# The corner block of a triangular inverse by two TensorE passes in two of the step bodies, and a rearranged first step

## The chip, the cores and the metric

The kernel runs on one core of a Trainium2 chip. The metric is the device time of one launch in microseconds, the median of several runs. All data are float32 unless a line says otherwise.

## The reference

One layer: a delta-rule attention over chunks, and behind it a mixture of experts with a shared part. What matters here is the first half, cut to the lines that the change touches:

```python
# q, k, v: silu of a causal convolution over 4 tokens of x @ W; beta = sigmoid(x @ Wb)
A = jnp.einsum('bhncd,bhnmd->bhncm', k_beta, k)
M = jnp.where(stril, A, 0.0) + jnp.eye(chunk)
u = solve_triangular(M, v_beta, lower=True)
w = solve_triangular(M, k_beta, lower=True)
def step(S, inp):
    u_i = u_i - w_i @ S
    o_i = q_i @ S + tril(q_i @ k_i.T) @ u_i
    S = S + k_i.T @ u_i
# B, T, D, H = 2, 1024, 512, 16; dk = 32
# then: norm of o by head, o @ Wo, residual; router, 32 experts with 4 of them per token, shared part, norms
```

The solves are with unit lower triangular matrices. The kernel takes chunks of 32 tokens, forms the inverse of each matrix once and multiplies by it.

## The kernel before

**Staging.** The tokens are taken in 8 steps of 128 tokens of both batches (256 columns). The program has a set-up part, body 0, bodies 1 to 8, a closing body 9, and then, behind a barrier of all engines, the expert part. Body s prepares step s on VectorE (DVE) and ScalarE (ACT): convolutions, silu, grams, and the inverses of its 128 x 4 triangular matrices. In the same body TensorE (PE) runs the core of step s-1: four sub-steps j = 0 to 3, each of a state matmul (L497), a solve (L512: inverse times residual), a state update (L520) and an output matmul (L526). Between these four, `fill` puts pieces of other work, written out by hand in `FILL` and `FILLS`: one letter is one piece, X turn of x, B betas, G one gram (L481), P half a projection (L468, step s+1), W output projection (L549, step s-2), O output squares (L539), R router, E and F first halves of the shared part, V and Y its second half, H turn of h. `FILL` has 16 slots; slot 4j+m stands behind operation m of sub-step j. Slot 13 is "PP", slot 14 is empty, slot 15 is "EEEEOEEEE". In bodies 1 and 7 the letters of steps that don't exist drop out: body 1 has no W, E, F, V, Y; body 7 has no X and P.

**The ring.** The pieces write to six PSUM banks in turn. `all_jobs` lists the jobs in TensorE's order, a job's bank is its number modulo 6, and `wait_free` waits until the job six before has been released.

**The inverse.** A matrix of 32 x 32 is held on each of the 128 partitions for each of the entries in `inv`. `masks` (L975) copies a gram from PSUM with the upper triangle kept, `problems` (L983) turns them, `row_weights` and `column_weights` scale, and `inverse_diagonal` (L1012) solves the two diagonal blocks of 16 x 16. The block below them, the corner, is minus the second inverse times the block times the first inverse: `turn_first` (L1021), `below_times_first` (L1032, products of 8 x 16 x 16 and 8 x 16 x 8) and `second_times` (L1038, the same sizes), each a product by `tensor_tensor` (L1028) and a sum by `tensor_reduce` (L1030) on VectorE. `inverse_by_token` (L1043) turns the result into `invT` and signals `inv_ready`, for which the solve of the next core waits at j = 0.

**The order at the end of a body** is fixed on VectorE: state j = 2, column weights, the copy of `turn_first`, moments of x, residual j = 3 (L1067), the two products of `below_times_first`, state j = 3 (L1071), turn of k, `output_sums` (L1077), the two products of `second_times`, `scale_output` (L1084), `inverse_by_token`; then residual j = 0 of the next body. On ScalarE: copies of projections and solves, the output's copy (L728) and square (L733), `output_norm` (L736).

**Body 0** has no core. TensorE projects step 0 (L633), waiting for `consts`, which GpSimd signals at the end of its constants; then betas, the four grams, the turn of x, and all twelve P. VectorE convolves k, takes moments, convolves q, multiplies k, turns it, scales x, multiplies q, convolves v, masks. ScalarE copies banks 0 to 3, then the sigmoid factor of k, bank 4, that of q, bank 5, moments, betas, that of v, x. At its end VectorE scales the output weights `wo` by `onw` (L1204).

Of the kernel before, what the change touches and what calls it, by code (L numbers as in the profile page):

```python
# [26 lines left out]
P = 128  # L27
# [33 lines left out]
PIECES = dict(X=1, H=1, O=1, G=4, P=12, W=8, E=8, F=8, V=4, Y=4)  # L61
BANKS = dict(X=2, H=2, O=2, G=4, P=6, W=2, E=2, F=2, V=1, Y=1)

FILL = ["BXRWW", "WWW", "WWW", "PP", "GPP", "GFF", "GFF", "GFF", "FFPP", "HPP", "PP", "VVVV", "YYYY", "PP", "", "EEEEOEEEE"]
FILLS = {0: ["BGGGGXPPPPPPPPPPPP"],
         STEPS: ["RWWW", "WWW", "WW", "F", "FF", "F", "F", "FF", "FH", "VV", "V", "VY", "YYY", "EE", "E", "EEOEEE"], STEPS + 1: ["RWWWWWWWWFFFFFFFFHVVVVrYYYYEEEEEEEE"]}


def step_of(body, section):

    if section in "XP":
        return body + 1
    if section in "BG":
        return body
    if section == "O":
        return body - 1
    if section in "WHEr":
        return body - 2
    return body - 3


def pieces_of(body):

    done = dict.fromkeys("BRrXHOGPWEFVY", 0)
# [29 lines left out]
class Ring:  # L114
# [17 lines left out]

    def full(self, *job):
# [6 lines left out]
def step_part(nc, ctx, dram, shared):  # L140
# [24 lines left out]
    upto = sb("upto", [P, CH])  # L165
    eps_l2 = sb("eps_l2", [P, 1])
# [25 lines left out]
    mid_cols = sig[:, 2, HB * HB:2 * HB * HB].rearrange("p (c j) -> p c j", c=HB)  # L192

# [66 lines left out]
    halo_done = sem("halo_done")  # L260
    kq_ready = sem("kq_ready")
# [34 lines left out]
    act_step = sem("act_step")  # L296

# [87 lines left out]
    def _(pool):  # L385
# [8 lines left out]
        g.memset(upto[:, :], 1.0)  # L394
        g.memset(pre[:, :, :, 0:HALO], 0.0)
# [37 lines left out]
    def _(pe):  # L433
# [39 lines left out]
        def gram(s, j):  # L473
# [9 lines left out]
            m.then_inc(ring.full("G", s, j), 1)  # L483

# [117 lines left out]
        def fill_for(body):  # L602
# [3 lines left out]
            def fill(at):  # L606
                for c, step, n in slots[at]:
# [10 lines left out]
                    elif c == "G":  # L618
                        gram(step, n)
                    elif c == "P":  # L620
# [23 lines left out]
    def _(act):  # L644
# [46 lines left out]
        def take_projection(s, n):  # L691
# [13 lines left out]
            release("P", s, n)  # L705
            if half == 1:
# [11 lines left out]
        def key_norms(s):  # L718
# [3 lines left out]
            sc_e.activation(knorm[:, :], knorm[:, :], ACT.Exp, scale=0.5).then_inc(knorm_ready, 1)  # L722

# [91 lines left out]
        for n in range(BANKS["P"]):  # L815
            take_projection(1, n)
        end_steps()

        def body(s):
# [10 lines left out]
            if new:  # L830
                silu_factor(s, 1)
                silu_factor(s, 0)
# [37 lines left out]
            if nxt:  # L870
                take_projection(s + 1, 5)
            take_output(core, 3)
# [79 lines left out]

# [912 lines left out]
```

## Time and profile before

| | |
|---|---|
| median of 3 runs | 963.0 us (961.36 to 964.35) |
| profiled execution | 962.78 us, its span 961.0 us |
| PE, weight loads, DVE, ACT, POOL busy | 822.5, 629.2, 661.5, 364.8, 116.7 us |
| mean granted clock of TensorE | 0.934 of full speed |
| body 0 | up to 86 us |
| body 1, first residual to first residual of body 2 | 85.96 to 155.75 us |
| body 7, in the same way | 536.62 to 611.84 us |
| expert part | from 703.4 us |

Times of rows are microseconds from the start of the span. Busy shares are of the whole span; what one stage waits for is read from the timelines. The time before an instruction in which its engine was idle stands in brackets at the end of its row, with what ended it; "issue" is idle time in which the engine waited for nothing that the profile shows.

### The profile page before, as it was taken

What the parts mean: (1) busy time and instruction counts of PE and PEld (TensorE: products, weight loads), DVE (VectorE), ACT (ScalarE), POOL (GpSimd) and SP (SyncE); (2) the same over time, 40 slices, a digit from 0 to 9 for tenths busy, and PEclk for the clock granted to TensorE, in tenths of its full rate; (3) what the DMA queues carried; (4) which work ended last, traced back from release to release, by engine and by line L of the source; (5) the groups of instructions that cost most, each with busy time, mean ns of one, the idle gap of its engine ahead of it and who ended that gap; (6) DMA issues with size and microseconds to landing.
All of it is one profiled execution on the core that took longest, in us unless ns stands there. A gap on an engine that the chain in (4) does not pass through costs nothing. (4 is left out here: it accounts for less than half of the span.)

```text
span 961.0 us, 30663 instructions
## 1 busy us (share of the span) xinstructions
PE 822.5 (86%) x13456; PEld 629.2 (65%) x13456; DVE 661.5 (69%) x1220; ACT 364.8 (38%) x683; POOL 116.7 (12%) x173
## 2 busy tenths in 40 slices
PE   6794779789999999999999787998779999999910
PEld 5683665676777777687687464666566887788800
DVE  2799699799789789879877988787691222222238
ACT  2605334435534644544554451332321222222215
POOL 2000000000000000000000000000002454544345
PEclk9895988999999999999999987998889999999965
DMA  8301004300101021020020020020176999999376
GB/s 307 72 23 47 3 3 168 108 3 25 62 18 39 3 69 27 24 70 23 4 69 24 3 70 23 2 89 2 48 286 220 362 362 346 344 360 358 96 266 278
DMA packets 49632, 113.09 MB, mean 118 GB/s; under 512 B 8688, under 2 KB 8816, under 8 KB 49504
## 3 DMA queue, kind: packets, MB, share of 16 engines
q1 hardware_dynamic: 44384, 100.70, 29.1%
q0 software_dynamic: 5120, 10.49, 4.8%
q8 instruction: 104, 1.70, 0.7%
q14 instruction: 24, 0.20, 0.1%
HBM read 84.34 MB, written 26.84 MB: 116 GB/s over the span
## 5 line engine op out<-in xcount | busy, mean ns | idle before, releaser
L468 PE MATMUL bank<-xnT,wring 128*128 128x256 f32 x768 | 183.6, 396 | 2.1 <-ACTq L681 1.3
L468 PEld LDWEIGHTS bank<-xnT,wring 128*128 128x128 f32 x768 | 149.3, 198 | 24.9 <-ACTq L681 1.5
L587 PE MATMUL bank<-late,ffn_w 128*128 128x256 f32 x480 | 117.3, 394 | 0.0
L1754 DVE TENSOR_TENSOR hid<-ps_g,sg 128x160 f32<-128x160 f32 x32 | 10.4, 324 | 148.5 <-ACT sg L1650 148.5
L942 DVE SCALAR_TENSOR_TENSOR cv<-pre,taps,cv 128x1024 f32<-128x1024 f32 x72 | 92.4, 1283 | 18.1 <-ACTq L707 14.4
L587 PEld LDWEIGHTS bank<-late,ffn_w 128*128 128x128 f32 x480 | 90.8, 195 | 15.2 <-issue 1.1
L1509 POOL MEMSET xgT<- 128x512 f32 x2 | 1.0, 532 | 686.9 <-POOLq L1834 686.9
L1609 PEld LDWEIGHTS ps_g<-xgT,wring 128*128 128x128 f32 x640 | 74.4, 192 | 10.9 <-issue 10.9
L1609 PE MATMUL ps_g<-xgT,wring 128*128 128x128 f32 x640 | 74.8, 275 | 1.3 <-ACT xgT L1640 1.3
L1640 ACT ACTIVATE xgT<-ps_x 128x320 f32<-128x320 f32 x32 | 14.0, 437 | 132.8 <-PE ps_x L1598 132.8
L549 PE MATMUL bank<-wo,o_ch 128*128 128x512 f32 x128 | 60.1, 605 | 0.6 <-DVE o_ch L1086 0.6
L481 PE MATMUL bank<-kq 32*32 32x64 f32 x2048 | 42.8, 233 | 16.7 <-DVEq L961 9.1
L598 PE MATMUL bank<-ffn_w,late 128*128 128x512 f32 x112 | 54.5, 628 | 0.1
L703 ACT ACTIVATE pre<-bank 128x512 f32<-128x512 f32 x48 | 28.6, 597 | 67.2 <-PE bank L468 63.7
L481 PEld LDWEIGHTS bank<-kq 32*32 32x32 f32 x2048 | 36.6, 117 | 20.3 <-DVEq L961 11.0
L512 PEld LDWEIGHTS bank<-resid,invT 32*32 32x32 f32 x2048 | 22.0, 110 | 39.9 <-issue 39.8
L512 PE MATMUL bank<-resid,invT 32*32 32x32 f32 x2048 | 25.5, 199 | 24.2 <-DVE resid L1069 24.1
L497 PEld LDWEIGHTS bank<-kq,state 32*32 32x32 f32 x2048 | 32.3, 110 | 20.8 <-issue 11.9
L497 PE MATMUL bank<-kq,state 32*32 32x64 f32 x2048 | 37.7, 224 | 8.4 <-DVE state L1075 7.8
L726 ACT ACTIVATE unew<-bank 128x256 f32<-128x256 f32 x32 | 12.3, 384 | 68.7 <-PE bank L512 68.1
L1618 PE MATMUL ps_y<-wring,hid 128*80 128x512 f32 x80 | 37.7, 593 | 0.2 <-DVE hid L1756 0.2
L980 DVE TENSOR_TENSOR grams<-bank,upto 128x512 f32<-128x512 f32 x32 | 21.8, 682 | 23.0 <-PE bank L481 22.1
(202 smaller groups left out, 1474.2 us busy)
## 6 DMA issues: line engine op xcount, KB each, us to landing
wring<-in_ffn_W_gate SPq DMA_DIRECT2D x20, 512.0 KB, 7.6
wring<-in_ffn_W_up SPq DMA_DIRECT2D x20, 512.0 KB, 9.6
wring<-in_ffn_W_down SPq DMA_DIRECT2D x20, 512.0 KB, 10.7
x_in<-in_attn_x SPq DMA_DIRECT2D x8, 512.0 KB, 3.7
x_res<-in_attn_x SPq DMA_DIRECT2D x8, 512.0 KB, 4.8
side_rows<-late SPq DMA_DIRECT2D x8, 512.0 KB, 7.0
x_rows<-x SPq DMA_DIRECT2D x8, 512.0 KB, 3.2
h_rows<-h SPq DMA_DIRECT2D x8, 512.0 KB, 4.4
```

The lines of the kernel that those rows point to most:

```text
L468: m = te.matmul(bank[:, c * COLS:(c + 1) * COLS], wqkv[:, w, kt, ct * P:(ct + 1) * P], xnT[:, kt, :], start=(kt == 0), stop=(kt == KT - 1))
L481: m = te.matmul(bank[quad(hh), i * 64:(i + 1) * 64], kq[quad(hh), i * J + j, 0, :], kq[quad(hh), i * J + j, :, :].rearrange("p a c -> p (a ...
L497: m = te.matmul(here[quad(hh), i * 64:(i + 1) * 64], now[quad(hh), i, :], kq[quad(hh), i * J + j, :, :].rearrange("p a c -> p (a c)"), sta ...
L512: m = te.matmul(aside[quad(hh), i * DK:(i + 1) * DK], invT[quad(hh), i * J + j, :], resid[quad(hh), i, :], start=True, stop=True)
L549: m = te.matmul(bank[:, :], o_ch[:, ct * B + b, :], wo[:, ct, :], start=(ct == 0), stop=(ct == CT - 1))
L587: m = te.matmul(bank[:, c * COLS:(c + 1) * COLS], w[:, kt, ft * P:(ft + 1) * P], hT[:, kt, :], start=(kt == 0), stop=(kt == KT - 1))
L598: m = te.matmul(bank[:, :], sh_h[:, ft, b * TT:(b + 1) * TT], sd_w[:, ft, :], start=(ft == 0), stop=(ft == FT - 1))
L703: sc_e.activation(pre[:, w, 4 * half:4 * half + 4, HALO:], bank, ACT.Copy)
L942: link(v.scalar_tensor_tensor(out=out, in0=pre[:, w, :, n:n + TT], scalar=taps[:, w, n:n + 1], in1=out, op0=ALU.mult, op1=ALU.add))
L980: link(v.tensor_tensor(both, bank, upto[:, :].rearrange("p (a i c) -> p a i c", i=1, a=1).to_broadcast([P, 2, I8, CH]), ALU.mult))
L1609: m = te.matmul(ps_g[q % 2][:, (2 * a + i) * P:(2 * a + i + 1) * P], w[:, k, i * P:(i + 1) * P], xgT[q % 2][:, k, :], start=(k == 0), stop ...
L1618: m = te.matmul(ps_y[q % 2][0:CAP, :], hid[q % 2][:, i, :], w_down[q][:, i, :], start=(i == 0), stop=(i == 1))
```

## The change

**Bodies 1 and 7** (`BLOCKS = (1, 7)`). `masks` keeps only the two diagonal blocks of k's gram for the inverse and writes the corner apart, by a second operation. `turn_first`, `below_times_first` and `second_times` go. Instead VectorE turns the diagonal inverses twice, by rows (`turn_rows`, where `turn_first` stood) and by token (`turn_diagonal`, behind state j = 3). TensorE gets two passes of 128 matmul calls each with 16 columns: Q (`corner_times_first`) in slot 14, between the state update and the output matmul of j = 3, and S (`second_times_middle`) in slot 15 behind the output squares, ahead of the next body's state matmul. ScalarE copies Q's result (`take_middle`), and VectorE adds S's to `invT` (`join_corner`) behind `scale_output` and signals `inv_ready` there. Q and S take one job each of the ring.

**Body 0.** The convolutions of k and q are made in halves, the first half of each as soon as the first of its two banks is copied; VectorE's and ScalarE's orders are changed as the diff shows. `wo` is scaled by ScalarE, behind `key_norms` and ahead of the copies of step 1's projections, which no longer wait for `rstd(0, 2)` but for the last of them. Body 0 keeps the old corner.

**Constants.** GpSimd makes masks `blocks` and `above`: two fills more ahead, and in the loop over four quadrants five operations more, each waited for, ahead of `consts`.

```diff
+BLOCKS = (1, 7)
+for body in BLOCKS:
+    if body > 0:
+        FILLS[body] = FILL[:14] + ["Q", "OS" if body == 1 else "EEEEOSEEEE"]
...
+    inv_rows = sig[:, 0, :].rearrange("p (g c) -> p g c", c=CH)
+    corner = sig[:, 1, :].rearrange("p (g c) -> p g c", c=CH)
+    middle = sig[:, 2, :].rearrange("p (g c) -> p g c", c=CH)
...
+            for a in range(2):
+                alone(g.affine_select(out=blocks[quad(n), a, :], in_=blocks[quad(n), a, :], compare_op=ALU.is_ge, fill=0.0,
+                                      base=0, pattern=[[1, CH]], channel_multiplier=-1))
+            alone(g.affine_select(out=blocks[quad(n), 0, HB:CH], in_=blocks[quad(n), 0, HB:CH], compare_op=ALU.is_ge, fill=0.0,
+                                  base=-HB, pattern=[[0, HB]], channel_multiplier=1))
+            alone(g.memset(above[quad(n), HB:CH], 1.0))
+            alone(g.affine_select(out=above[quad(n), HB:CH], in_=above[quad(n), HB:CH], compare_op=ALU.is_ge, fill=0.0,
+                                  base=HB - 1, pattern=[[0, HB]], channel_multiplier=-1))
...
+        def corner_times_first(s):
+            pe.wait_ge(inverse_turned, 2 * BLOCKS.index(s) + 1)
+            ring.wait_free(pe, "Q", s, 0)
+            bank = ring.bank("Q", s, 0)
+            for n in range(G):
+                for hh in range(HT):
+                    m = te.matmul(bank[quad(hh), n * HB:(n + 1) * HB], corner[quad(hh), n, :], inv_rows[quad(hh), n, 0:HB], start=True, stop=True)
+            m.then_inc(ring.full("Q", s, 0), 1)
+        def second_times_middle(s):
+            ring.wait_taken(pe, "Q", s, 0)
+            pe.wait_ge(inverse_turned, 2 * BLOCKS.index(s) + 2)
+            ring.wait_free(pe, "S", s, 0)
...
+                    m = te.matmul(bank[quad(hh), n * HB:(n + 1) * HB], middle[quad(hh), n, :], invT[quad(hh), n, HB:CH], start=True, stop=True)
+            m.then_inc(ring.full("S", s, 0), 1)
...
+        def take_middle(s):
+            ring.wait_full(act, "Q", s, 0)
+            link(sc_e.activation(middle[:, :, 0:HB], ring.bank("Q", s, 0)[:, :].rearrange("p (g c) -> p g c", c=HB), ACT.Copy))
+            release("Q", s, 0)
...
-        for n in range(4):
+        for n in range(3):
             take_projection(0, n)
         silu_factor(0, 1)
+        take_projection(0, 3)
+        rstd(0, 1)
+        silu_factor(0, 0)
         take_projection(0, 4)
-        silu_factor(0, 0)
         take_projection(0, 5)
-        rstd(0, 1)
         take_beta(0)
+        take_x(1)
         silu_factor(0, 2)
-        take_x(1)
         key_norms(0)
-        rstd(0, 2)
+        act.wait_ge(small_in, 16 * SMALL)
+        act.wait_ge(weights_in, 16 * 4)
+        for ct in range(CT):
+            last = sc_e.activation(wo[:, ct, :], wo[:, ct, :], ACT.Copy, scale=onw[:, 0:1])
+        last.then_inc(wo_scaled, 1)
         for n in range(BANKS["P"]):
+            if n == BANKS["P"] - 1:
+                rstd(0, 2)
             take_projection(1, n)
...
+            if s in BLOCKS:
+                v.tensor_tensor(both, bank, blocks[:, :, :]..., ALU.mult)
+                link(v.tensor_tensor(corner..., bank[:, 0], above[:, :]..., ALU.mult))
...
+        def turn_rows():
+            link(v.transpose(inv_rows.rearrange("p g c -> p c g"), inv.rearrange("p j k -> p k j")))
+            link(v.memset(middle[:, :, HB:CH], 0.0))
+            dve.sem_inc(inverse_turned, 1)
+        def turn_diagonal():
+            link(v.transpose(invT[:, :, :].rearrange("p g c -> p c g"), inv))
+            dve.sem_inc(inverse_turned, 1)
+        def join_corner(s):
+            ring.wait_full(dve, "S", s, 0)
+            link(v.tensor_tensor(invT[:, :, HB:CH], invT[:, :, HB:CH], ring.bank("S", s, 0)[:, :].rearrange("p (g c) -> p g c", c=HB), ALU.add))
+            dve.sem_inc(ring.free("S", s, 0), 1)
+            dve.sem_inc(inv_ready, 1)
...
-        conv(0, 1, 0)
+        for half in range(2):
+            conv_half(0, 1, half)
+        halo(1, 0)
         first_moments(1)
-        conv(1, 0, 0)
+        conv_half(1, 0, 0)
         silu_kq(0, 1, 0)
+        conv_half(1, 0, 1)
+        halo(0, 0)
         turn_k(0)
...
-        for ct in range(CT):
-            last = v.tensor_scalar(wo[:, ct, :], wo[:, ct, :], onw[:, 0:1], None, ALU.mult)
-        last.then_inc(wo_scaled, 1)
```

## Rows read from the trace of the kernel before

**Rows 1.** The page: busy time of each engine; the instruction packets among the queues.

```profile
PE 822.5 (86%) x13456; PEld 629.2 (65%) x13456; DVE 661.5 (69%) x1220; ACT 364.8 (38%) x683; POOL 116.7 (12%) x173
...
q8 instruction: 104, 1.70, 0.7%
```

**Rows 2.** Timeline of GpSimd in the set-up; columns: start, us, engine, line, out<-in.

```profile
5.60 0.21 POOL L420 TENSOR_SCALAR_AFFINE_SELECT upto<-upto 32x32 f32<-32x32 f32 x1
5.88 0.29 POOL L423 TENSOR_SCALAR_AFFINE_SELECT before<-before 128x128 bf16<-128x128 bf16 x1
```

**Rows 3.** Timeline of TensorE in body 0: projection of step 0 and the grams.

```profile
10.72 23.02 PE L468 MATMUL bank<-xnT,wring 128*128 128x256 f32 x96 [0.85 <-issue]
...
40.03 6.41 PE L481 MATMUL bank<-kq 32*32 32x64 f32 x256 [4.46 <-DVEq L961]
```

**Rows 4.** Timeline of VectorE in body 0 and at the start of body 1.

```profile
28.20 3.93 DVE L942 SCALAR_TENSOR_TENSOR cv<-pre,taps,cv 128x1024 f32<-128x1024 f32 x3 [0.82 <-ACTq L707]
...
47.83 1.93 DVE L985 STREAM_TRANSPOSE inv_pad<-grams 128x1024 f32<-128x1024 f32 x1
...
84.37 1.67 DVE L1205 TENSOR_SCALAR wo<-wo,onw 128x512 f32<-128x512 f32 x4 [0.23 <-DVE invT L1044]
85.96 0.44 DVE L1068 STREAM_TRANSPOSE resid<-bank 128x256 f32<-128x256 f32 x1
```

**Rows 5.** Timeline of ScalarE in body 0.

```profile
23.91 0.68 ACT L704 ACTIVATE cv<-bank,taps 128x512 f32<-128x512 f32 x1
...
28.24 1.06 ACT L668 ACTIVATE sig<-cv 128x1024 f32<-128x1024 f32 x1 [0.19 <-ACT cv L704]
...
72.09 0.29 ACT L663 ACTIVATE rs<-mv,eps_ln 128x2 f32<-128x2 f32 x1 [21.53 <-DVE mv L919]
```

**Rows 6.** Timeline of VectorE in body 1 and at the start of body 2.

```profile
113.10 0.69 DVE L980 TENSOR_TENSOR grams<-bank,upto 128x512 f32<-128x512 f32 x1 [2.88 <-PE bank L481]
...
131.72 0.38 DVE L1023 COPY sig<-inv_pad 128x256 f32<-128x256 f32 x1
...
134.42 2.29 DVE L1028 TENSOR_TENSOR sig<-sig,inv_pad 128x2048 f32<-128x2048 f32 x1
...
141.23 1.22 DVE L1030 TENSOR_REDUCE sig<-sig 128x128 f32<-128x1024 f32 x1
...
155.75 0.45 DVE L1068 STREAM_TRANSPOSE resid<-bank 128x256 f32<-128x256 f32 x1 [0.24 <-DVE invT L1044]
```

**Rows 7.** TensorE, end of body 1: timeline; then a stretch: PE busy, PEclk, DMA.

```profile
140.34 0.72 PE L520 MATMUL bank<-unew,k_tok 32*32 32x32 f32 x62
...
145.37 3.78 PE L539 MATMUL bank<-o_r,headsm 128*128 128x256 f32 x8 [3.72 <-DVE o_r L1082]
149.08 1.93 PE L497 MATMUL bank<-kq,state 32*32 32x64 f32 x64
...
156.81 0.74 PE L512 MATMUL bank<-resid,invT 32*32 32x32 f32 x64 [1.00 <-DVE resid L1069]
...
145.30:149.10 3.80, 3.73 (x11) 0.50 0.02 4
```

**Rows 8.** Timeline of TensorE in body 1: two pauses on "issue" among the grams.

```profile
108.49 0.93 PE L481 MATMUL bank<-kq 32*32 32x64 f32 x52 [1.43 <-issue]
...
112.06 0.93 PE L481 MATMUL bank<-kq 32*32 32x64 f32 x52 [1.84 <-issue]
```

**Rows 9.** Timeline of TensorE at the end of body 7 and in body 8.

```profile
590.82 0.75 PE L512 MATMUL bank<-resid,invT 32*32 32x32 f32 x64
...
594.26 0.52 PE L526 MATMUL bank<-grams,unew 32*32 32x32 f32 x37 [1.24 <-issue]
...
599.96 1.89 PE L539 MATMUL bank<-o_r,headsm 128*128 128x256 f32 x8
...
612.89 0.74 PE L512 MATMUL bank<-resid,invT 32*32 32x32 f32 x64 [1.10 <-DVE resid L1069]
```

**Rows 10.** Timeline of VectorE in body 2: the last mask.

```profile
184.47 0.69 DVE L980 TENSOR_TENSOR grams<-bank,upto 128x512 f32<-128x512 f32 x1 [2.91 <-PE bank L481]
```

More of the change, by code:

```diff
@@ L165, in step_part @@
     upto = sb("upto", [P, CH])
+    blocks = sb("blocks", [P, 2, CH])
+    above = sb("above", [P, CH])
     eps_l2 = sb("eps_l2", [P, 1])
@@ L394, in _ @@
         g.memset(upto[:, :], 1.0)
+        g.memset(blocks[:, :, :], 1.0)
+        g.memset(above[:, :], 0.0)
         g.memset(pre[:, :, :, 0:HALO], 0.0)
@@ L483, in gram @@
             m.then_inc(ring.full("G", s, j), 1)
+        def corner_times_first(s):
[10 more added lines that the diff above has]
+            ring.wait_free(pe, "S", s, 0)
+            bank = ring.bank("S", s, 0)
+            for n in range(G):
+                for hh in range(HT):
+                    m = te.matmul(bank[quad(hh), n * HB:(n + 1) * HB], middle[quad(hh), n, :], invT[quad(hh), n, HB:CH], start=True, stop=True)
+            m.then_inc(ring.full("S", s, 0), 1)
         def core(s, fill):
@@ L619, in fill @@
                         gram(step, n)
+                    elif c == "Q":
+                        corner_times_first(step)
+                    elif c == "S":
+                        second_times_middle(step)
                     elif c == "P":
@@ L705, in take_projection @@
             release("P", s, n)
+            if s == 0 and half == 0:
+                act.sem_inc(pre_half, 1)
             if half == 1:
@@ L831, in body @@
                 silu_factor(s, 1)
+            if new:
                 silu_factor(s, 0)
@@ L951, in conv_end, with halo, conv_half @@
             dve.sem_inc(conv_done[w], 1)
+            halo(w, s)
+        def halo(w, s):
             link(v.tensor_copy(pre[:, w, :, 0:HALO], pre[:, w, :, TT:TT + HALO]))
             dve.sem_inc(halo_done, 1)
+        def conv_half(a, w, half):
+            i = slice(4 * half, 4 * half + 4)
+            if half == 0:
+                dve.wait_ge(pre_half, a + 1)
+            else:
+                dve.wait_ge(pre_ready[w], 1)
+            for n in range(TAPS - 1):
+                link(v.scalar_tensor_tensor(out=cv[:, w, i, :], in0=pre[:, w, i, n:n + TT], scalar=taps[:, w, n:n + 1], in1=cv[:, w, i, :], op0=ALU.mult, op1=ALU.add))
+            if half == 1:
+                dve.sem_inc(conv_done[w], 1)
         def silu_kq(a, w, s):
@@ L979, in masks @@
             both = grams[:, 0:2 + s % 2:1 + s % 2, :, :].rearrange("p a (i j) c -> p j a i c", j=J)[:, j]
-            link(v.tensor_tensor(both, bank, upto[:, :].rearrange("p (a i c) -> p a i c", i=1, a=1).to_broadcast([P, 2, I8, CH]), ALU.mult))
+            if s in BLOCKS:
+                v.tensor_tensor(both, bank, blocks[:, :, :].rearrange("p a (i c) -> p a i c", i=1).to_broadcast([P, 2, I8, CH]), ALU.mult)
+                link(v.tensor_tensor(corner.rearrange("p (i j) c -> p j i c", j=J)[:, j], bank[:, 0], above[:, :].rearrange("p (i c) -> p i c", i=1).to_broadcast([P, I8, CH]), ALU.mult))
+            else:
+                link(v.tensor_tensor(both, bank, upto[:, :].rearrange("p (a i c) -> p a i c", i=1, a=1).to_broadcast([P, 2, I8, CH]), ALU.mult))
             dve.sem_inc(ring.free("G", s, j), 1)
@@ L1211, in body @@
             new = s < STEPS
+            here = new and s not in BLOCKS
             residual(core, 0)
@@ L1269, in body @@
             residual(core, 3)
-            if new:
+            if here:
                 below_times_first(0)
@@ L1273, in body @@
                 first_scale(s + 2)
-            if new:
+            if here:
                 below_times_first(1)
@@ L1284, in body @@
             output_sums(core)
-            if new:
+            if here:
                 second_times(0)
@@ L1288, in body @@
                 hidden_gate(last, 0)
-            if new:
+            if here:
                 second_times(1)
@@ L1293, in body @@
             scale_output(core)
+            if s in BLOCKS:
+                join_corner(s)
             if last >= 0:
                 hidden_up(last, 0)
-            if new:
+            if here:
                 inverse_by_token()
```

49 lines of the change are left out of this document (33 added, 16 removed).

## Prediction

> **What bounds the kernel now.** I read the page first. TensorE is busy in 86% of the span and VectorE in 69% [rows 1], but these are averages over a step part, where the delta rule runs, and an expert part that starts only when the step part has ended on every engine. The change touches the step part alone, so what it is worth is decided there and is handed on one to one. The timelines of each engine through body 0, the ends of bodies 1 and 7, and the starts of the bodies behind them then show who waits for whom.
>
> In body 0 the two engines take turns until the grams: VectorE's convolutions wait for ScalarE's copies, ScalarE's sigmoid waits for a whole convolution, and the grams start at 40.03 [rows 3, 5]. From the transpose at 47.83 VectorE works almost without a gap up to the residual at 85.96 [rows 4], while ScalarE sits idle for 21.5 us [rows 5]. So VectorE sets the end of body 0.
>
> In bodies 1 and 7 VectorE also works without a gap from the last mask on: products of 2.29 us and 1.22 us each [rows 6]. But TensorE is only just ahead of it. After the output squares at 145.37 it goes on without idle time through the state matmuls, betas, the turn of x and the first output projection, and reaches the solve of the next core at 156.81 after 1.00 us of waiting [rows 7]. Behind that point TensorE leads: in body 2 VectorE waits 2.91 us for the last gram [rows 10], and from 156.81 to that gram TensorE's own waits on other engines sum to 0.6 us. The reader is to see that time saved on VectorE in body 1 is worth at most 1 us unless TensorE arrives earlier too, and that time added to TensorE is passed on nearly whole.
>
> One more limit matters. A run of small matmuls stalls on "issue": 52 grams start at 108.49 after 1.43 us and 52 at 112.06 after 1.84 us, with exactly 128 matmuls (and 128 weight loads) from one to the other [rows 8]. The chip moved 104 instruction packets, 1.70 MB, so 16 KB each [rows 1]. I read this as a stream that arrives in blocks of 128 pairs, and 3.57 us as the least time between two blocks that are both waited for. In body 7 a block that was entered freely, 27 pairs into the solve at 590.82, was followed by the next one at 594.26 [rows 9], which is 3.15 us. I take 3.15 us for the first and 3.9 for each next block; 3.57 and 4.1 are the ends of what I see for the latter.
>
> The Trainium skill ("Runtime: NRT & Kernel Launch", Instruction fetch mechanics) says that fetch comes in blocks of 256 instructions, and that it is hidden because instructions are issued more slowly than they arrive. The trace agrees with the block and disagrees with the hiding. By the rule of the Trainium skill the sum would be that of the second case below.
>
> **Body 0: halves, constants and the output weights.** GpSimd gets 16 more selects and 4 more fills, each behind the wait for the one before. A select takes 0.28 us from start to start [rows 2] and a fill less, so 20 take at most 5.6 us and, with the fills shorter, some 5.1; the constants that were ready at 6.17 are ready near 11.3. TensorE began to project at 10.72 [rows 3] and waits for them: +0.6 us (0.5 to 1.0), on the path, because the first bank is what all wait for.
> The third bank is copied by 24.59 [rows 5]. Now the sigmoid of k follows at once: three times 1.06 with gaps, to 28.0. The fourth bank takes to 29.2. The second half of q's convolution takes 2.2 (half of 3.93 is 1.96 [rows 4], and 0.2 for three more fixed costs, an estimate), to 31.6; the sigmoid of q runs to 35.0, the product to 36.4. The grams start 3.4 us earlier. Less comes through: banks five and six are copied only behind that sigmoid, to 37.4, and v's convolution and the masks follow one another to 45.3, where the transpose started at 47.83. That is 2.5 us.
> The output weights leave VectorE: 1.67 us and the 0.2 before them [rows 4], 1.8 us. On ScalarE four passes cost about 4 x 0.68 = 2.7 us inside its 21.5 us of idle time [rows 5]; their loads landed long before. Without that cover they would cost those 2.7 us. Sum of body 0: -2.5 - 1.8 + 0.6 = **-3.7** (-2.5 to -4.4).
>
> **Body 1: what VectorE loses.** Two products of 2 x 2.29 and two of 2 x 1.22, with gaps 14.2 us, and the copy at 131.72, 0.42 [rows 6]. Added: four mask halves of some 0.4 each (0.69 for twice the elements), of which three fall into waits and the last is on the path behind the gram that it waited 2.88 us for [rows 6]; one more transpose (1.93 [rows 4]); a fill of 512 elements, 0.1 to 0.6, taken as 0.4, near the 0.38 of the 256-element copy; the join, 0.7. VectorE has some 11 us less to do. But before the last residual it has 0.4 + 1.95 + 0.45 - 0.4 = 2.4 us more, and that residual releases the chain on TensorE.
> **Body 1: the first pass (Q).** It stands between the state update at 140.34 and the output matmul. So it is in front of the output copy, its square, the sums, the output squares and, through them, everything. It is 128 calls, 256 pairs. Its lower bound is the small solve, 64 pairs in 0.74 [rows 7]: four of them in one stream with half the columns are some 2.4 us, an estimate. Its upper bound is the grams, 256 pairs in 6.41 [rows 3], plus stalls. Counting pairs from the stall at 112.06 puts a block's start at the fifth pair of the state update. Shifted by 2.4, that is 142.8. The next block comes at 145.95, the one behind it at 149.85; 61 pairs of Q and 64 of the output matmul are left, 1.6 us. The output matmul ends at 151.4, where it ended at 141.65: 7.35 us for Q.
> **Body 1: the squares and the second pass (S).** Output copy, square and sums take 3.3 us from there as before (0.4, 1.06, 1.23 and the steps between), VectorE being free. The squares start at 154.75 instead of 145.37. TensorE has idled for 3 us as before, where its granted clock was 0.50, 1.2 GHz [rows 7], so I take the 3.78 us of that row and not the 1.89 of the one in body 7 [rows 9]: 158.5. S crosses one block freely after 119 pairs (2.0) and then waits 3.15: 163.65. The state matmuls stand behind it, 1.93 and the rest of S: 165.8. VectorE's residual was released by then at 155.75 [rows 6], so VectorE is 10 us late; and betas, turn of x and projection follow as before (from 151.01 to 155.81), 4.9 us with the step to the next, so that the solve starts at 170.8 instead of 156.81. Less 0.6 us of idle time in body 2: **+13.4** (without stalls 4.4 to 6.8; with full clock 10).
> The ring banks of later jobs turn by two (Q and S), which moves no release that anyone waits for.
>
> **Body 7** by the same steps. The last residual is late by 1.4 but hidden behind the shared projection, so the solve is late by 0.4 only. Block starts at 591.5, 594.7, 598.6, 602.5: the output matmul ends at 602.9 instead of 594.8. Eight matmul groups of E (5.4 at low clock) still come before the squares, which start at 608.3 instead of 599.96 [rows 9]; 1.89, S 4.55, the rest of E 3.6, state 1.1, router 2.05, projection 2.84. The solve starts at 623.4 instead of 612.89: **+10.5** (2.3 to 4 without stalls). In body 8 VectorE waits for TensorE, so this stays.
>
> Sum against the profiled run: 962.8 (span 961.0 and 1.8 around it; the median is 963.0) - 3.7 + 13.4 + 10.5 = **983**.
>
> **The cases.**
> 1. As summed, 983; own range 975 to 989. For it: the stalls come back in nearly every body where groups of 64 pairs follow one another, 17 gaps in the trace. Against it: nobody has run 16 columns there, and the grams of body 0 ran 256 pairs in 6.41 us, 3.2 per block, without a gap [rows 3]. Chance 0.55.
> 2. No stalls in Q and S: they cost 2.4 to 4 us each. Body 1 gives +5.6, body 7 +3.2: 962.8 - 3.7 + 8.8 = 968. Against it are the stalls just named. Chance 0.22. The rule of the Trainium skill on fetch, named above, would make this case the likeliest.
> 3. Faster. VectorE's own order sets the next body, and TensorE's fill behind the state matmuls is slack after all. If Q and S are 2.4 us each and the squares run at full clock (1.89), the residual of the next core starts at 155.2 in body 1 instead of 155.75 and at 610.3 in body 7 instead of 611.84: -0.5 - 1.5 - 3.7 gives 957. It decides where Q and S together stay under 5 us in body 1; against it is that TensorE led after 156.81. Chance 0.15.
> 4. The two effects cancel within 0.3% (what a measurement of this kernel can tell from no change): stalls smaller and clock higher than I take them, 963. Chance 0.08.
>
> **Numbers.** The range takes cases 1, 2 and 4: 960 to 989, which leaves out nearly all of case 3 and tails of case 1. Faster by over 0.3% has 0.16, within 0.3% 0.08, slower 0.76.
>
> **What would show it.** In the changed profile: first projection near 11.4; grams of body 0 near 37.2; the first residual near 82.3; ScalarE's four passes before 53; "issue" gaps of 1 to 3 us inside both new groups, 128 pairs apart; the first of them about 7 us long, gap included; VectorE idle for several microseconds at the end of bodies 1 and 7; solve of the next core 10 us later than body 0's gain would have it. The prediction is wrong if the new groups run through in under 3 us, if the solve in body 2 starts at the old time less 3.7, or if body 0 gains nothing, because then the halves wait for banks all the same.

## The result, and the profile after

| | before | after |
|---|---|---|
| median | 962.18 us (957.74 to 964.35) | 982.73 us (980.01 to 983.98) |
| profiled execution, its span | 962.78, 961.0 | 982.47, 980.7 |
| mean granted clock of TensorE | 0.934 | 0.927 |

The ratio is 1.0208, 95% interval 1.0182 to 1.0234: slower by 20 us, where 983 us had been predicted. The sum was right; two of its three terms were not, and that their errors nearly cancel is luck.

The page of after, beside [rows 1]: VectorE has 19.5 us less to do, TensorE 11.3 us more, and the chip moved 112 instruction packets instead of 104.

```profile
PE 833.8 (85%) x14480; PEld 638.9 (65%) x14480; DVE 642.0 (65%) x1218; ACT 368.3 (38%) x689; POOL 121.0 (12%) x195
...
q8 instruction: 112, 1.84, 0.8%
```

**Body 0.** TensorE's and VectorE's timelines of after, the rows that answer to [rows 3, 4]: first projection, grams, first transpose, first residual. Then ScalarE's four passes over the output weights.

```profile
11.87 22.41 PE L495 MATMUL bank<-xnT,wring 128*128 128x256 f32 x96 [2.03 <-POOL before L450]
...
37.06 3.48 PE L508 MATMUL bank<-kq 32*32 32x64 f32 x233 [0.96 <-DVEq L1047]
41.70 0.53 PE L508 MATMUL bank<-kq 32*32 32x64 f32 x23 [1.15 <-issue]
```

```profile
46.02 1.99 DVE L1075 STREAM_TRANSPOSE inv_pad<-grams 128x1024 f32<-128x1024 f32 x1
...
82.64 0.45 DVE L1174 STREAM_TRANSPOSE resid<-bank 128x256 f32<-128x256 f32 x1 [0.23 <-DVE invT L1150]
```

```profile
48.72 2.54 ACT L877 ACTIVATE wo<-wo,onw 128x512 f32<-128x512 f32 x4
```

The grams start 2.97 us earlier and the transpose 1.81; with the output weights gone from VectorE the first residual comes 3.32 us earlier (82.64 against 85.96). Some 0.6 us of each is not the change's: the projection starts 1.15 us later, behind the longer constants, but took 22.41 us in this execution and 23.02 in that of before [rows 3].

**Body 1.** TensorE from the last state update to the solve of body 2, in the place of [rows 7]. Q is L519 (197 + 58 + 1 matmuls), S is L530 (252 + 4).

```profile
140.58 1.82 PE L519 MATMUL bank<-sig 32*32 32x16 f32 x197
144.44 0.96 PE L519 MATMUL bank<-sig 32*32 32x16 f32 x58 [2.04 <-issue]
...
145.26 1.08 PE L574 MATMUL bank<-grams,unew 32*32 32x32 f32 x61
149.35 3.78 PE L587 MATMUL bank<-o_r,headsm 128*128 128x256 f32 x8 [3.02 <-DVE o_r L1188]
153.06 3.60 PE L530 MATMUL bank<-invT,sig 32*32 32x16 f32 x252
157.97 0.29 PE L530 MATMUL bank<-invT,sig 32*32 32x16 f32 x4 [1.31 <-issue]
158.09 1.93 PE L545 MATMUL bank<-kq,state 32*32 32x64 f32 x64
159.95 2.68 PE L482 MATMUL bank<-xnT,wb_h 128*16 128x256 f32 x8
...
165.30 0.75 PE L560 MATMUL bank<-resid,invT 32*32 32x32 f32 x64
```

And VectorE in the same stretch, in the place of [rows 6]: the products are gone and it now waits, 3.64 us for ScalarE's square of the output, 6.86 us for the output norm, then for S and for the state matmuls.

```profile
148.07 1.22 DVE L1188 SCALAR_TENSOR_TENSOR o_r<-q_sq,o_r 128x1024 f32<-128x1024 f32 x1 [3.64 <-ACT o_r L793]
156.15 1.23 DVE L1192 TENSOR_TENSOR o_ch<-o_ch,o_r 128x1024 f32<-128x1024 f32 x1 [6.86 <-ACTq L804]
158.29 0.69 DVE L1145 TENSOR_TENSOR invT<-invT,bank 128x512 f32<-128x512 f32 x1 [0.91 <-PE bank L530]
160.08 0.45 DVE L1174 STREAM_TRANSPOSE resid<-bank 128x256 f32<-128x256 f32 x1 [1.10 <-PE bank L545]
```

**Body 7.** TensorE, in the place of [rows 9]. Four pauses on "issue" stand in Q, the output matmul behind it and S, and the shared part behind S (L635) takes 6.26 us.

```profile
600.88 1.35 PE L519 MATMUL bank<-sig 32*32 32x16 f32 x128 [1.02 <-issue]
604.35 1.52 PE L519 MATMUL bank<-sig 32*32 32x16 f32 x99 [2.12 <-issue]
...
607.82 0.75 PE L574 MATMUL bank<-grams,unew 32*32 32x32 f32 x38 [1.54 <-issue]
608.50 5.49 PE L635 MATMUL bank<-late,ffn_w 128*128 128x256 f32 x16
613.83 1.89 PE L587 MATMUL bank<-o_r,headsm 128*128 128x256 f32 x8
615.65 1.79 PE L530 MATMUL bank<-invT,sig 32*32 32x16 f32 x192
619.62 1.05 PE L530 MATMUL bank<-invT,sig 32*32 32x16 f32 x64 [2.17 <-issue]
620.60 6.26 PE L635 MATMUL bank<-late,ffn_w 128*128 128x256 f32 x16
...
632.37 0.75 PE L560 MATMUL bank<-resid,invT 32*32 32x32 f32 x64
```

**Where the time went.** The starts of the residuals (the transpose by which VectorE takes each state matmul), in every kernel minus before, say where a difference arises and whether it stays. One column is one kernel; the kernels other than after are those of the experiments.

| residual, start in before | after | halves_only | no_corner17 | body1_only | body7_only | half_calls |
|---|---|---|---|---|---|---|
| body 1, 85.96 | -3.3 | -3.5 | -4.1 | -2.7 | -1.7 | -2.2 |
| body 2, 155.75 | +4.3 | -0.7 | -2.9 | +6.4 | -0.9 | +3.5 |
| body 3, 228.74 | +8.6 | -1.4 | -3.5 | +11.5 | -1.0 | +2.8 |
| body 3, j = 2, 263.90 | +6.6 | -3.4 | -5.4 | +11.5 | -1.6 | +2.3 |
| body 7, 536.62 | +6.3 | -3.5 | -5.0 | +11.3 | -1.8 | +2.1 |
| body 8, j = 1, 621.84 | +19.5 | -2.5 | -5.8 | +11.8 | +12.7 | +5.5 |

In after: -3.3 us by the end of body 0, +9.6 between the starts of bodies 1 and 7, and +13.2 in body 7, behind which the difference stays (+19.5, and 19.7 in the two spans).

### The profile page after: what moved, and what is told of

The parts are those of the page before. It is cut to its first block and busy times, and to the rows that moved or that the text cites. A ratio compares the mean times of both kernels' runs of the same rounds, so it can differ in the third digit from the quotient of the medians.

```text
span 980.7 us, 32746 instructions
## 1 busy us (share of the span) xinstructions
PE 833.8 (85%) x14480; PEld 638.9 (65%) x14480; DVE 642.0 (65%) x1218; ACT 368.3 (38%) x689; POOL 121.0 (12%) x195
## 5 line engine op out<-in xcount | busy, mean ns | idle before, releaser
L635 PE MATMUL bank<-late,ffn_w 128*128 128x256 f32 x480 | 119.1, 399 | 0.0
L635 PEld LDWEIGHTS bank<-late,ffn_w 128*128 128x128 f32 x480 | 92.0, 198 | 15.6 <-issue 1.1
L1013 DVE SCALAR_TENSOR_TENSOR cv<-pre,taps,cv 128x1024 f32<-128x1024 f32 x66 | 84.7, 1283 | 4.7 <-ACTq L761 1.3
L508 PE MATMUL bank<-kq 32*32 32x64 f32 x2048 | 38.3, 220 | 13.6 <-issue 7.9
L508 PEld LDWEIGHTS bank<-kq 32*32 32x32 f32 x2048 | 32.5, 107 | 16.6 <-issue 9.3
L597 PEld LDWEIGHTS bank<-wo,o_ch 128*128 128x128 f32 x128 | 22.5, 190 | 20.8 <-issue 20.1
```

Source lines behind the costliest of these rows:

```text
L508: m = te.matmul(bank[quad(hh), i * 64:(i + 1) * 64], kq[quad(hh), i * J + j, 0, :], kq[quad(hh), i * J + j, :, :].rearrange("p a c -> p (a ...
L597: m = te.matmul(bank[:, :], o_ch[:, ct * B + b, :], wo[:, ct, :], start=(ct == 0), stop=(ct == CT - 1))
L635: m = te.matmul(bank[:, c * COLS:(c + 1) * COLS], w[:, kt, ft * P:(ft + 1) * P], hT[:, kt, :], start=(kt == 0), stop=(kt == KT - 1))
L1013: link(v.scalar_tensor_tensor(out=out, in0=pre[:, w, :, n:n + TT], scalar=taps[:, w, n:n + 1], in1=out, op0=ALU.mult, op1=ALU.add))
```

## The experiments

**Body 0's part alone, and each body alone.** All three are made from the changed kernel, by its own list of bodies. Without any body in it the two masks go from the constants as well.

```diff
-BLOCKS = (1, 7)
+BLOCKS = ()      # halves_only
+BLOCKS = (1,)    # body1_only
+BLOCKS = (7,)    # body7_only
```

> Only body 0 as in the change; no body uses the two passes, and the two masks for them are not made. My account of the change: body 0 gives about 3.3 us (the first residual came at 82.64 instead of 85.96) and the missing constants another 0.5, so 3.8 us under the kernel before, about 958.5, and all later bodies keep the old pace, the first residual near 82.1. Rival, that the early gain of body 0 is taken back by a later wait as the bodies fall into step: no difference from before, 962.

Measured 959.97 us, ratio 0.9957 (0.9929 to 0.9986). Its span is 958.5 against 961.0. The interval just leaves out 1, so this version is faster than both kernels, by little (the medians of the two are 2.2 us apart): body 0's part is worth having, the corner passes are not. The ratio fits the account (958.5) and not the rival (962).

Its column shows a gain of 3.5 us at the end of body 0, of which 0.7 is left at body 2 and 3.4 again late in body 3. No pass runs in this kernel, so the dip isn't theirs, and the rows show most of it. In body 1 TensorE waits 2.30 us ahead of a gram, and the projection behind that gram takes 5.41 us; in before the wait is 1.11 us (ahead of 99.94) and the projection takes 3.72. This is 1.7 of the 2.2 us lost up to the residual j = 2. TensorE's timeline of halves_only:

```profile
96.50 1.09 PE L498 MATMUL bank<-kq 32*32 32x64 f32 x64 [2.30 <-DVEq L1037]
97.52 5.41 PE L485 MATMUL bank<-xnT,wring 128*128 128x256 f32 x16
```

In body 3 it is the other way round. The second to fourth gram of before stop on "issue" for 0.99, 0.28 and 0.19 us, and those of halves_only run through: 5.2 us against 3.1 for the three. TensorE's timeline of before, the first of these stops:

```profile
249.81 0.53 PE L481 MATMUL bank<-kq 32*32 32x64 f32 x22 [0.99 <-issue]
```

After and no_corner17 have no such stops there either, and gain the same 2 us in the middle of body 3, so the passes' price is read against halves_only and not against before. Why the stops stand in one trace and not in the other is open: TensorE has as many matmuls in halves_only as in before.

> The change with the two passes in body 1 alone. My account: body 1 costs what the traces show between its first residual and that of body 4, +9.8 us, so 962.2 - 3.3 + 9.8 = 969; residuals up to body 6 as in the changed kernel (6.3 us late), and no further loss in body 7. Rival, that the two bodies interact through the ring and the position of the instruction stream: outside 967 to 971.

> The change with the two passes in body 7 alone. My account: body 7 costs 12.9 us by the traces (residuals 6.3 us late before it, 19.2 behind it), of which my prediction had 10.5, so 962.2 - 3.3 + 12.9 = 972. Dropping body 1's passes takes away 1024 TensorE instructions, four whole blocks of 256, so the pauses on issue should stay where they are in body 7. Rival, that body 7 was worse only because body 1 had run late before it: under 970.

Measured 972.89 (1.0109, 1.0082 to 1.0136) and 974.46 (1.0123, 1.0079 to 1.0167): 12.9 and 14.5 us above halves_only. Body 7 alone is near its expectation of 972, and its pauses stand at the same matmuls as in after. Body 1 alone lies above its range of 967 to 971, on the side that the rival had, and the two together cost 27.4 where after has 22.8. TensorE's timeline of body1_only, same place as in after:

```profile
146.28 0.98 PE L519 MATMUL bank<-sig 32*32 32x16 f32 x58 [2.71 <-issue]
...
160.07 0.29 PE L530 MATMUL bank<-invT,sig 32*32 32x16 f32 x4 [2.44 <-issue]
...
162.06 3.60 PE L482 MATMUL bank<-xnT,wb_h 128*16 128x256 f32 x8
```

The pauses fall behind the same matmuls but last 0.67 and 1.13 us longer, and the betas behind them run 0.9 us longer. With a body 1 that starts 0.65 us later this covers the 2.1 us by which body 2 comes later than in after, and the 2.9 us at body 3. The other 2 us stand in body 3's grams: body1_only stops there as before does, for 1.02, 0.29 and 0.20 us, and after does not. The price of a pass is thus not a constant: with the same code in it, body 1 cost 9.6 us in one trace and 14 in the other. Each kernel has one trace, so whether this belongs to the build or to the execution isn't shown; the ten runs of body1_only lie between 967.8 and 975.75.

**Is it the place?** Q goes ahead of the last projection, where TensorE used to wait for VectorE's residual, and S goes ahead of the output squares, where it waits for the sums.

```diff
-FILLS[body] = FILL[:14] + ["Q", "OS" if body == 1 else "EEEEOSEEEE"]
+FILLS[body] = FILL[:12] + ["Q", "PP", "", "SO"]      # BLOCKS = (1,); ScalarE's copy of Q moved with it
```

> Passes in body 1 alone, the first moved to slot 12, where TensorE waited 4.9 us for the residual of j = 3, the second put ahead of the output squares, where it waited 3.0 us. If the place of the passes in the chain is what costs, the output matmul of j = 3 ends near 141.5 instead of 146.3 and the squares start near 147 instead of 149.35; body 1 then costs 4 to 6 us instead of 9.8, total 963 to 965. If instead the passes cost by their TensorE time wherever they stand, the total stays near 969. If VectorE's saving of 11 us could be had at all once they are covered, it would be under 958.

Measured 968.94 (1.0075, 1.0048 to 1.0103): 9.0 us above halves_only, 4 below body1_only. TensorE's timeline:

```profile
135.94 3.07 PE L519 MATMUL bank<-sig 32*32 32x16 f32 x214 [1.88 <-DVEq L1136]
140.29 0.77 PE L519 MATMUL bank<-sig 32*32 32x16 f32 x42 [1.28 <-issue]
...
151.21 1.28 PE L530 MATMUL bank<-invT,sig 32*32 32x16 f32 x133 [1.92 <-issue]
154.57 1.89 PE L530 MATMUL bank<-invT,sig 32*32 32x16 f32 x123 [2.07 <-issue]
156.38 3.78 PE L587 MATMUL bank<-o_r,headsm 128*128 128x256 f32 x8
```

The first pass fills a wait now, but the three pauses (5.3 us) and 7.0 us of matmuls come along, and VectorE stands 9.53 us ahead of the last state addition. The place saves 4 of 12.9 us, no more, and the two intervals overlap: the 969 of the case in which the passes cost their time on TensorE wherever they stand.

**Columns or instructions?** few_cols keeps all 128 calls of each pass and cuts 16 columns to 4 (the other columns of the corner are left out). half_calls does the opposite: 64 calls of 32 columns (every second problem's corner is not computed rightly there). S is changed in the same way as Q.

```diff
-m = te.matmul(bank[quad(hh), n * HB:(n + 1) * HB], corner[quad(hh), n, :], inv_rows[quad(hh), n, 0:HB], ...)
+m = te.matmul(bank[quad(hh), n * HB:n * HB + 4], corner[quad(hh), n, :], inv_rows[quad(hh), n, 0:4], ...)              # few_cols
+for n in range(0, G, 2): te.matmul(bank[quad(hh), n * HB:(n + 2) * HB], ..., inv_rows[quad(hh), n, :], ...)           # half_calls
```

> The changed kernel with 4 of the 16 columns in each matmul of both passes; the corner's other columns are left out, so the corner is not computed whole. Same number of instructions. If the passes are limited by the arrival of instruction blocks, almost nothing changes: 980 to 983, and the pauses on issue stay. If they are limited by the array's work, three quarters of some 21 us go in the part that scales with columns: 967 to 972.

> The changed kernel with half the calls in both passes, each of 32 columns instead of 16, so the array streams as many columns with half the instructions; every second problem takes the place of its neighbour, so the corner is not computed rightly. If instruction blocks are the limit, the pauses of 2.04 and 1.31 us in body 1 and of 1.02, 2.12 and 2.17 in body 7 go or shrink, with half of the time per pair: 965 to 971. If columns are the limit, it stays at 980 to 983. If it is a fixed time per matmul without the blocks, half of the 10.6 us that the pairs themselves take goes: 976 to 978.

few_cols measured 984.38 (1.0234, 1.0193 to 1.0274): a quarter of the columns saves nothing. half_calls measured 968.22 (1.0051, 1.0018 to 1.0084): the same number of columns in half the matmuls is 14.5 us faster than after. TensorE in body 1, of few_cols and then of half_calls; the last two rows of the second fence are from its body 7.

```profile
142.92 1.80 PE L519 MATMUL bank<-sig 32*32 32x4 f32 x197
146.79 0.64 PE L519 MATMUL bank<-sig 32*32 32x4 f32 x57 [2.07 <-issue]
...
159.30 0.27 PE L530 MATMUL bank<-invT,sig 32*32 32x4 f32 x4 [2.28 <-issue]
```

```profile
145.49 1.25 PE L519 MATMUL bank<-sig 32*32 32x32 f32 x126
...
153.99 1.29 PE L530 MATMUL bank<-invT,sig 32*32 32x32 f32 x128
...
607.97 1.29 PE L530 MATMUL bank<-invT,sig 32*32 32x32 f32 x128
609.19 3.72 PE L635 MATMUL bank<-late,ffn_w 128*128 128x256 f32 x16
```

197 matmuls take 1.80 us with 4 columns and 1.82 with 16, and the pause behind them is 2.07 and 2.04. What a pass costs is its number of matmuls (128 calls are 256): their own time, the pauses on "issue" 128 matmuls apart, and the low clock behind them. Half of the matmuls' own time would have given the 976 to 978 of the third case, so the pauses and the clock hold the larger part. That the pauses are waits for the next block of instructions is read from the packets, and no run changes the fetch alone: 104 packets in before, 106 with 256 matmuls more (moved1_half, below), 108 with 512 more (body1_only, half_calls), 112 with 1024 more. With half the calls a pass takes 1.3 us and both of body 1 run through without a pause. In body 7 two pauses stay, in Q and in the output matmul, as one does there in before [rows 9]; the one in S is gone, and the shared part behind it takes 3.72 us in place of 6.26. By the table body 1 costs 4.3 us there and body 7 3.4 (TensorE's solve in body 8 stands at 618.42, at 632.37 in after and 612.89 in before).

The two ways combined, in body 1 alone: the moved place with 64 calls per pass.

> The passes in body 1 alone, at the moved place (first pass ahead of the last slots, second pass ahead of the output norms), and each pass in 64 matmuls of 32 columns in place of 128 of 16; of the 32 columns one half lands on the neighbour's place, so every second problem's corner is left wrong. Moved with 128 matmuls it measured 968.9, with 64 each in bodies 1 and 7 at the old places 968.2. If the passes cost what TensorE spends on them and the pauses on issue: some 2.5 us of matmuls and no pause, 1 to 2 us for the residual that comes late, so 961 to 964 with the pauses gone. If the place costs by itself, whatever the passes' length: 966 to 969. If VectorE's saving pays as soon as the passes are short: below 957.

Measured 962.8 (0.999, 0.9966 to 1.0014). The kernel before, run beside it, had 963.8, and 962.2 beside moved1 and halves_only, so the ratios are compared: against 1.0075 with 128 calls at the same place, half the calls are worth 8 us (6 by the medians); against the 0.9957 of halves_only the passes still cost some 3. A pause of 1.91 us is left in S. VectorE has 10 us less to do in this kernel than in halves_only (busy 651.7 against 661.4), and nothing of it shows in the time.

**What is the most that a pass could win?** Leaving VectorE's corner products out, with nothing in their place, prices the gain apart from the cost (the corner block of the inverse is left out of the computation there).

```diff
-here = new and s not in BLOCKS      # VectorE's products, and nothing else, depend on it
+here = new and s not in SKIP        # BLOCKS = (), SKIP = (1, 7): no_corner17;  SKIP = 1 to 8: no_corner_all2
```

> The kernel with the body 0 part alone (halved step one, output weights on ScalarE, no passes on TensorE), and with VectorE's corner products left out in bodies 1 and 7 and nothing in their place; the computation leaves out the off-diagonal corner of the inverse there. It prices what the passes could win at most. My theory: VectorE is not what bodies 1 and 7 wait for. TensorE's idle before the residual that follows the corner is 1.0 to 1.1 us in each body and the projections stand behind it, so some 14 us less of VectorE gives 1 us each at most: 957 to 960 beside 960 of the body 0 part alone. Rival, VectorE sets the pace of these bodies: 14 us less for each, 932 to 936. A part of it, as where the state's solve starts earlier and the body's own end follows: 945 to 952.

> VectorE's corner products left out in all eight bodies from body 1 on, with nothing in their place (the corner of the inverse is left out of the computation); masks as the changed kernel has them in bodies 1 and 7. It asks what VectorE's corner work is worth anywhere. My theory: TensorE is busy for some 75 of 77 us in bodies 2 to 6, so those bodies give 1 to 2 us each at most, and bodies 1 and 7 1 us each: 948 to 958. Rival, VectorE's work is in the path of every body: 14 us less in each of eight, near 850 to 880. If nothing of it is in the path: 959 to 961.

no_corner17 measured 956.18 (0.9934, 0.991 to 0.9959), which is 0.0023 or 2.2 us below halves_only (3.8 by the medians); the intervals of the two overlap. The profiled executions differ by 3.3 us at the late residual of body 8: 2.2 at body 2, then 1.5 to 2 up to body 7, then 3.3. But 0.7 us of this stood at the first residual already, ahead of anything that the edit touches. VectorE lost 28.5 us of work (661.4 to 632.9). TensorE and VectorE at the end of body 1:

```profile
150.80 1.98 PE L588 MATMUL bank<-wo,o_ch 128*128 128x512 f32 x4
153.90 0.74 PE L551 MATMUL bank<-resid,invT 32*32 32x32 f32 x64 [1.11 <-DVE resid L1166]
```

```profile
149.52 1.23 DVE L1183 TENSOR_TENSOR o_ch<-o_ch,o_r 128x1024 f32<-128x1024 f32 x1 [6.12 <-ACTq L795]
150.66 1.95 DVE L1141 STREAM_TRANSPOSE invT<-inv_pad 128x1024 f32<-128x1024 f32 x1
152.84 0.45 DVE L1165 STREAM_TRANSPOSE resid<-bank 128x256 f32<-128x256 f32 x1 [0.23 <-DVE invT L1141]
```

VectorE idles 6.12 us ahead of the output's scaling, which waits for ScalarE's norm, and that for TensorE's squares. The 14 us went into waits. no_corner_all2 measured 947.54 (0.9833, 0.9801 to 0.9865), just below the 948 to 958 expected: six more bodies are worth 10 us by the ratios (the kernel also makes the two masks again), 1.6 us each, for 71 us less of VectorE's work (632.9 to 561.9). In no body does VectorE's corner stand in the path for more than 2 us or so.

**The output weights by themselves**, scaled on ScalarE in the kernel before:

```diff
+        for ct in range(CT):        # ScalarE, behind key_norms(0)
+            last = sc_e.activation(wo[:, ct, :], wo[:, ct, :], ACT.Copy, scale=onw[:, 0:1])
-        for ct in range(CT):        # VectorE, behind inverse_by_token
-            last = v.tensor_scalar(wo[:, ct, :], wo[:, ct, :], onw[:, 0:1], None, ALU.mult)
```

> The kernel before with one edit: the output weights are scaled on ScalarE behind the key norms. The first residual of body 1 should start 1.5 to 1.8 us earlier than 85.96, near 84.3. If the four passes on ScalarE held up its copies of the next projections and with them the moments of x, the gain would be lost and the residual stay near 86.

VectorE's timeline in body 0 of this kernel:

```profile
48.50 1.95 DVE L990 STREAM_TRANSPOSE inv_pad<-grams 128x1024 f32<-128x1024 f32 x1
...
85.11 0.45 DVE L1073 STREAM_TRANSPOSE resid<-bank 128x256 f32<-128x256 f32 x1 [0.24 <-DVE invT L1049]
```

Measured 959.28 (0.9969, 0.9948 to 0.999). In the profiled execution the first residual comes only 0.85 us earlier. Its first rows show why: the transpose that opens VectorE's stretch is 0.67 us later than in [rows 4], because the projection of step 0 took 23.77 us where it took 23.02 [rows 3], before anything of the edit had run. From that transpose to the residual VectorE takes 36.61 us where it took 38.13, and after takes 36.62. So the output weights are worth 1.5 us.

The projection's length moves body 0's end as a whole. It is 22.41 to 24.04 us in the eight kernels that have body 0 and the constants as after has them (all but before, wo_only, halves_only and no_corner17). The start of the first residual less that length is 60.0 to 60.3 us in all eight, so their gains over before are 1.7 to 3.3 us, and after, with the shortest projection, has the largest. At before's 23.02 us body 0 gains 2.7. By the same difference before has 62.94, wo_only 61.34, halves_only 58.95 and no_corner17 58.86: at equal projections the output weights are worth 1.6, the halves 2.4, and the constants cost 1.3. In the total, wo_only's 0.9969 and halves_only's 0.9957 can't be told apart, so what the halves are worth is shown by these rows alone.

## Why the prediction was right, step by step

**What bounds the kernel: right.** TensorE leads at the ends of bodies 1 and 7, and VectorE's time there is worth little. The text said at most 1 us for body 1; no_corner17 is 1.5 us further ahead of halves_only at body 2 than at body 1, and 2.2 us (3.3 by the profiled executions) for both bodies. The reading was of the right kind and short by some 0.5 us in size, which one pair of traces doesn't tell from nothing.

**Body 0: right, in part by luck.** Predicted -3.7, measured -3.3, of which 0.6 is this execution's short projection: -2.7 at equal projections, inside the -2.5 to -4.4 named. Grams at 37.06 for 37.2, transpose 1.81 us earlier for 2.5, first residual at 82.64 for 82.3. By terms at equal projections: halves -2.4 for -2.5, output weights -1.5 for -1.8, constants +1.15 to +1.3 for +0.6. The constants are the term that was mis-sized: they were ready at 11.81 for the 11.3 predicted, the projection began 1.15 us late (11.87, where 11.4 was named), and that its first bank came only 0.54 us late is the short projection again. A pause on "issue" of 1.15 us now stands inside the four grams, which ran as one group before [rows 3]. Of the gain, 2.5 us arrive at the end (halves_only, last row of the table).

**Body 1: right in mechanism, 3.8 us too much.** Predicted +13.4, measured +9.6. The step that failed is the wait at the first of the two block borders in Q. The prediction counted pairs from the last pause, put block starts at 142.8, 145.95 and 149.85, and gave Q 7.35 us with two pauses. Q had one, 4.8 us from 140.58 to its last matmul, 2.5 less than predicted. In the prediction's frame, where body 1 starts as in before (add 3.32), the state update ahead of Q came 2.95 us late for 2.4, the output matmul ended at 149.7 for 151.4, the squares started at 152.7 for 154.75, and the solve at 168.6 for 170.8: 2.2 us in the end. S was right, 5.2 us in all for 5.15: the pause ended 4.9 us behind S's start, though the matmuls ahead of it took 3.60 (252 at a granted clock of 0.50) and the pause itself 1.31. The squares took the 3.78 us taken for them. The remaining 1.6 us: the prediction took 14.0 less 0.6; the rows show 11.8 at the solve and 9.6 in the end. This lies in the dip that halves_only has as well, the stops in body 3's grams that before has and after has not, and is no slack in body 2: against halves_only the passes of body 1 cost 9.2 us at the solve of body 2 and 9.8 at the start of body 7.

The borders themselves were counted rightly. The pause behind Q's 197th matmul puts the border before it 128 back, at the 69th, which the array (the part of TensorE that runs the matmuls) passed at some 141.2 without a stop. The instruction packets, of 16 KB, tell more. In after they start at 136.06, 142.07, 145.54, 150.57 and 155.59 us. The block that begins at the 69th can't have come with the packet at 142.07, which is later, so it came with that of 136.06 or an earlier one, 4 us or more ahead of need. The packet at 142.07 (1.07 us long, in by 143.1) starts 0.9 us behind that border and ends 1.3 us before TensorE resumes at 144.44, so it is taken as the one waited for. The packet at 136.06 starts 1 us behind the start of the last projection's 16 wide matmuls. That TensorE's sequencer, which reads the instructions, runs ahead of the array behind such slow matmuls, and so asks for blocks early, would explain it; no run tests this.

**Body 7: right in mechanism, 2.7 us too little.** Predicted +10.5, measured +13.2. With body 7's start shifted back by 6.32, TensorE resumed at 594.6, 598.0 and 601.5 where block starts were put at 594.7, 598.6 and 602.5 (3.47 us from one to the next, for 3.9), the squares came at 607.5 for 608.3, and S took 4.95 us for 4.55. The step that failed is "the rest of E 3.6": 16 matmuls of the shared part behind S took 6.26. The other differences nearly cancel: squares 0.8 early, S 0.4 more, the rows behind E 0.4 less, and a slip in the sum itself, whose terms come to 624.3 for the solve and not to the 623.4 that it states. The stretches of after and, for comparison, of half_calls (columns: window, length, PE busy, loads, VectorE, ScalarE, GpSimd, clock, DMA share, GB/s):

```profile
620.60:626.80 6.20, 6.20 (x23) 4.79 (x18) 0.69 (x1) 0.00 (x0) 0.00 (x0) 0.58 0.01 3
```

```profile
609.20:612.90 3.70, 3.70 (x26) 3.01 (x24) 1.76 (x2) 1.71 (x3) 0.00 (x0) 1.00 0.02 4
```

The granted clock was 0.58 behind the pause of 2.17 us in S, and 1.00 in half_calls, where S had none; 0.50 and 1.00 are the two levels, so most of the stretch ran at 1.2 GHz. The prediction priced the low clock in front of the squares (5.4 us for 5.49 measured) and did not carry the same step past S. Against the 3.62 us of the same matmuls in before this is 2.6 us. That the pause is what lowered the clock rests on these two kernels and on body7_only (2.12 us of pause in S, then 6.05 us); half_calls differs from after in S's matmuls too. TensorE in body 7 of before shows both lengths in one kernel, the first behind a pause of 1.24 us [rows 9]:

```profile
594.72 5.41 PE L587 MATMUL bank<-late,ffn_w 128*128 128x256 f32 x16
...
601.69 3.62 PE L587 MATMUL bank<-late,ffn_w 128*128 128x256 f32 x16
```

The granted clock was 0.68 in the first and 1.00 in the second.

**The rivals.** No stalls in Q and S (968 us) is excluded by the rows. half_calls lands on 968.2 but is not that case: it has half the matmuls, and two pauses are left in its body 7. VectorE's order as the bound (957) had as its condition that Q and S together stay under 5 us. In after they took 10. In body 1 of half_calls they took 2.5, and the body still cost time; no_corner17 and no_corner_all2 show how little VectorE's corner holds up at all. The two effects cancelling (963) is excluded by the 982.7. The Trainium skill ("Runtime: NRT & Kernel Launch", Instruction fetch mechanics), by which fetch in blocks of 256 instructions is hidden behind slower issue, agrees with the trace in the block's size (128 matmuls and 128 weight loads between the pauses that end at 600.88 and 604.35) and not in the hiding: those two pauses alone are 3.1 us.

**The signs named in advance** are there: gaps of 1 to 3 us inside both groups, 128 pairs apart, VectorE idle for several microseconds, and the four passes on ScalarE done by 51.3. The first group took 4.8 us in body 1 and 6.5 in body 7, for about 7.

## What to carry to other kernels

Price work that is moved to TensorE by its number of matmuls, not by its columns, and place the group where few small matmuls stand around it: 64 fewer calls per pass were worth 14.5 us over four passes, and 12 of 16 columns nothing. Before an engine is relieved, leave its work out once and see what that is worth: here 28.5 us of VectorE's time were worth 2 to 4 us, so no way of doing the corner elsewhere could have paid for more. Try the parts of a change alone: the part in body 0 is 0.43% faster than the kernel before, and the whole is 2.1% slower. Before a term is read from one row, see how far a row that the edit doesn't touch moves between traces: here it was 1.6 us.

## What was not expected of the hardware

- The length of a pass does not follow its columns: 9.2 ns per matmul with 16 columns and 9.1 with 4 (1.82 and 1.80 us for 197), and 10 with 32 (1.29 for 128).
- The same code pauses differently from trace to trace: at the same matmul of Q 2.04 us in after and 2.71 in body1_only, in S 1.31 and 2.44. In body 7, where two blocks in a row are waited for, the starts are 3.47 us apart in after and up to 4.02 in body7_only (594.03, 598.05).
- A pause costs twice. Behind the pause in S of body 7 the next 16 wide matmuls ran at a granted clock of 0.58 and took 2.6 us more than in before (6.26 and 3.62).
- Instructions can be there well ahead of the array: TensorE passed the border of a block at some 141.2, with no packet begun between 136.06 and 142.07.
